# A graph layer's sorting stage: row match ahead of column match in odd steps, on TensorE and on ScalarE

## The reference

```python
h = jnp.maximum(_layernorm(x, axis=-1), 0.0)
edge_in = jnp.concatenate([h[row], h[col], dist], axis=1)   # row = src, col = dst
e = jax.nn.silu(edge_in @ eW1 + eb1)                        # 129 -> 128
e = jax.nn.silu(e @ eW2 + eb2)                              # 128 -> 128
agg = jax.ops.segment_sum(e, row, num_segments=h.shape[0])
node_in = jnp.concatenate([h, agg], axis=1)
out = jax.nn.silu(node_in @ nW1 + nb1) @ nW2 + nb2
return x + out
```

## Time and profile before

| | us |
|---|---|
| median of 3 runs | 3083.42 (3081.98 to 3084.70) |
| the profiled execution | 3085.31 |
| its span, first to last instruction | 3083.5 |
| TensorE busy (matmul) | 2661.4 (86%) |
| VectorE busy | 2136.8 (69%) |
| GpSimd busy | 2017.5 (65%) |
| ScalarE busy | 1611.0 (52%) |
| mean granted clock of TensorE | 0.984 of full speed |

### The profile page before, as it was taken

One profiled execution on the slowest core, in us unless ns is written; L12 is line 12 of the kernel. 1 busy time (PEld: TensorE's weight loads), 2 busy tenths in 40 slices (PEclk: granted clock), 3 DMA queues, 4 the chain that ended last, 5 costly groups with the idle time before them and its releaser, 6 DMA issues.

```text
span 3083.5 us, 77463 instructions
## 1 busy us (share of the span) xinstructions
PE 2661.4 (86%) x21500; PEld 2104.6 (68%) x21800; DVE 2136.8 (69%) x7363; ACT 1611.0 (52%) x3444; POOL 2017.5 (65%) x2075
## 2 busy tenths in 40 slices
PE   6899999999688888888888888888888888888898
PEld 3455555555477777777777777777777777777787
DVE  8899999898566666666666666666666666666665
ACT  3677777777344444444444444444444444444443
POOL 1244444444677777777777777777777777777772
PEclk7999999999899999999999999999999999999998
DMA  3011111111222222222222222222222222222342
GB/s 93 19 32 33 39 26 38 27 38 24 43 59 59 59 59 59 58 59 59 59 59 59 58 59 59 59 59 59 57 59 59 58 60 59 57 58 55 76 124 92
DMA packets 366119, 171.82 MB, mean 56 GB/s; under 512 B 289558, under 2 KB 330190, under 8 KB 365998
## 3 DMA queue, kind: packets, MB, share of 16 engines
q0 software_dynamic: 69600, 123.49, 15.0%
q1 hardware_dynamic: 274206, 36.33, 7.7%
q10 hardware_dynamic: 22192, 10.53, 1.2%
HBM read 139.14 MB, written 31.04 MB: 55 GB/s over the span
## 4 chain that ended last, share of the span: by engine, by line
PE 75%; issue 13%; ACT 4%; DVE 4%; POOL 3%; DMA 1%; another core or an unknown queue 0%; DVEq 0%; ACTq 0%; SPq 0%; POOLq 0%
PE bk L1216 14%; PE bk L1236 14%; PE bk L1227 13%; PE bk L1214 9%; PE bk L1204 5%; PE bk L1079 4%; POOL GA L554 3%; PE bk L1113 2%; PE bk L1145 2%; ACT BIG L1355 2%; PE bk L1067 2%; PE bk L1284 1%; PE bk L1247 1%; PE bk L1225 1%; PE bk L1068 1%
## 5 line engine op out<-in xcount | busy, mean ns | idle before, releaser
L554 POOL DMA_INDIRECT GA<-q_d,IX x1758 | 1676.5, 954 | 549.1 <-issue 532.4
L921 DVE SCALAR_TENSOR_TENSOR GA<-c_bc,EW,GA 128x128 f32<-128x128 f32 x1758 | 558.9, 348 | 437.2 <-DMA GA<-q_d,IX 433.8
L930 DVE TENSOR_TENSOR BIG<-bk,BIG 128x128 f32 x1758 | 511.6, 291 | 376.6 <-issue 156.1
L1214 PE MATMUL bk<-identf,GA 128*128 128x128 f32 x1758 | 500.9, 285 | 257.2 <-issue 240.2
L1216 PE MATMUL bk<-OHS,P 128*128 128x128 bf16 x5274 | 692.4, 225 | 0.0
L1445 ACT ACTIVATE ED<-bk,eb1c 128x512 f32<-128x512 f32 x440 | 302.2, 687 | 701.4 <-PE bk L1216 691.3
L1216 PEld LDWEIGHTS bk<-OHS,P 128*128 x5274 | 501.6, 96 | 108.0 <-issue 0.2
L519 POOL DMA_INDIRECT rec_d<-BIG,GA x208 | 245.2, 1179 | 403.3 <-issue 307.4
L1236 PE MATMUL bk<-ED 128*128 128x128 f32 x3516 | 505.7, 287 | 0.0
L1227 PEld LDWEIGHTS bk<-W,ED 128*128 128x128 f32 x3516 | 464.6, 193 | 24.4 <-issue 7.6
L1227 PE MATMUL bk<-W,ED 128*128 128x128 f32 x3516 | 465.6, 276 | 12.0 <-issue 0.7
(11 more groups left out here) (249 smaller groups left out, 2743.0 us busy)
## 6 DMA issues: line engine op xcount, KB each, us to landing
GA<-q_d,IX POOLq DMA_INDIRECT x1758, 2.5
q_d<-QS SPq DMA_DIRECT2D x14, 448.0 KB, 3.1
u_d<-QS ACTq DMA_DIRECT2D x98, 64.0 KB
OHS<-u_d SPq DMA_DIRECT2D x18, 256.0 KB, 3.0
rec_d<-ED SPq DMA_DIRECT2D x16, 220.0 KB, 9.7
RW<-rec_d SPq DMA_DIRECT2D x110, 32.0 KB
rec_d<-BIG,GA POOLq DMA_INDIRECT x208
HT<-hT_d ACTq DMA_DIRECT2D x99, 32.0 KB
```

Of the source, the lines that this page charges most:

```text
L554: e.indirect_dma_start(G[k % 4 * U + u], None, q_d, bass.IndirectOffsetOnAxis(ap=IX[g // BG % 2][:, k * U + u:k * U + u + 1], axis=0))\
L921: ins = e.scalar_tensor_tensor(out=G[k % 4 * U + u], in0=c_bc[:, :], scalar=ew[:, w:w + 1], in1=G[k % 4 * U + u], op0=ALU.mult, op1=ALU.add)
L930: e.tensor_tensor(AGG[:, ds(v, P)], banks[6 + k % 2][:, u * P:(u + 1) * P], AGG[:, ds(v, P)], ALU.add).then_inc(s["ad"], 1)
L1214: e.matmul(z, G[k * U + u], identf[:, :], is_transpose=True, start=True, stop=False)
```

## The change

In odd steps the row match is written ahead of the column match on TensorE, and the row one-hot ahead of the column one-hot on ScalarE. Even steps have no column match, and read as before. No operation, buffer or semaphore is added or removed.

```diff
                 if 0 <= v - 2 < NR:
                     place(v - 2)
+                if 0 <= v < NR:
+                    matchrow(v)
                 if v % 2 == 1 and 0 <= v + 3 < NR:
                     matchcol((v + 3) // 2)
-                if 0 <= v < NR:
-                    matchrow(v)
                 if t == NSLOT:
...
                 if 12 <= t <= 20 and t % 2 == 0 and t != 18:
                     paired({12: 0, 14: 1, 16: 2, 20: 3}[t])
+                if 0 <= v < NR:
+                    rowhot(v)
                 if v % 2 == 1 and 0 <= v + 3 < NR:
                     colhot((v + 3) // 2)
-                if 0 <= v < NR:
-                    rowhot(v)
                 for f, q, b in node.get(t, ()):
                     f(q, b)
```

## The result

The changed kernel takes 3096.75 us (median of 5 runs, 3094.28 to 3098.91), against 3082.56 us before: 1.0046 times as long, 95% interval 1.0035 to 1.0057, 14.2 us. A second set of runs gave 3098.67 against 3081.63, 1.0056 (1.0042 to 1.0069), 17.0 us.

A forecast was written before the change was run, and what follows sets the result against it. TensorE and ScalarE together were taken to bound the sorting stage. Terms -8.9 + 16.0 + 5.6 = +12.7 us on the profiled 3085.3 gave 3098.0, forecast 3096 us since that run stood 1.9 above the median; 8 in 10: 3077 to 3107.

The forecast's parts named there:

- The bound: Sorting stage: TensorE and ScalarE set the pace together, VectorE follows with some 8% of room.
- The rule by busy share: Sorting stage: the engine with highest occupancy, VectorE at 88%, sets the time, so the sum would be 0.
- The gain of even steps, 8.9 of 33.1 us: Even steps' row matches idle 33.1 us; node matmuls waiting for ScalarE's earlier pieces let only 8.9 us be kept.
- the faster rival (3073): Even steps' stalls come back whole, node matmuls not holding TensorE: -31.7 + 21.6 = -10 us, 3073 us; chance 0.15.
- The transposes, 16.0 us: Bit transposes in even steps wait 52 times for the odd step's column one-hot, now later: 16.0 us lost.
- shifted by 0.49: Column one-hot ends 0.49 us later behind the row one-hot, so bit transposes right behind it go 0.49 later.
- The three that I took off beside ScalarE's squares: Transposes in steps 48, 108, 288: squares hold the next row match anyway, so 1.5 us came off the loss.
- Odd steps, 5.6 us: Column match now stands behind the row match's wait for the even step's row one-hot: 5.6 us lost.
- It evens out: Rival: VectorE and long ScalarE pieces swallow half of the losses, +2 us, 3085 us; chance 0.20.
- the clock rival: Stalls at the squares take the granted clock down twelve more times, 12 x 1.7 = 20 us, 3116 us; chance 0.05.
- The swap was there: Answers the rival that the swap isn't there, excluded since both engines' orders show it in each of 206 steps.
- The signs named: Sorting stage 8 to 18 us longer; waits at row match more than halved, at transposes, node matmuls and VectorE's reductions longer.

The follow-up runs named there:

- node_first_elsewhere: Kernel before, row ahead of column only in odd steps not before bit transposes, ScalarE's node pieces there between the one-hots: 3066.33 against 3081.63 us, 0.9952.
- act_only: Kernel before with its TensorE order kept, row one-hot ahead of column one-hot on ScalarE alone: 3117.79 against 3081.63 us, 1.0119.
- swap_elsewhere: Kernel before, row ahead of column on both engines in odd steps except those before bit transposes: 3588.68 against 3588.65 us, 1.0001; repeated, 0.9998.
- swap_before_bits: Kernel before, row ahead of column on both engines only in odd steps whose next step has bit transposes: 3602.85 against 3588.65 us, 1.0037.
- before_again: The kernel before, unchanged, run again for a profile, on chip 12: 3081.0 us.

## Why the prediction was right, and where it was not

- **The bound.** TensorE and ScalarE together, VectorE following: right. VectorE's waits for the ladders grew by 15.2 us with the stage, and shrank by 13 when it got shorter. The rule by busy share would have had the change, node_first_elsewhere and act_only level, since none of them changes VectorE's order; they moved the time by +14 to +17, -15 and +36 us.
- **The gain of even steps, 8.9 of 33.1 us.** The mechanism is shown: the subtraction comes at the same place with and without the row match's stall, and 0.47 sooner once the pieces are moved. Its size is not confirmed by itself. What lies outside the transposes came to -6.4 and -5.1 us in the two profiles, forecast -8.9+5.6 = -3.3; in time, swap_elsewhere was level. The node pieces are indeed what the faster rival (3073) would have needed out of the way: without the transposes' loss it had -31.7+5.6, 26 us faster, and node_first_elsewhere gives 15 of them.
- **The transposes, 16.0 us.** The right place, undersized: 21.5 and 20.8 us by the trace, 14 us (9 to 18) by swap_before_bits. Why the time on chip 1 shows less than the traces of the other kind stays open. The step that failed is "shifted by 0.49". That holds where the column match could start as TensorE arrived. Where the row match is late, the old column one-hot started beside it without waiting, and the new one stands behind both:

```profile
334.18 0.39 PE L1113 MATMUL bk<-GA,ED 128*128 128x512 bf16 x1 [0.64 <-ACT BIG L1355]
334.18 0.60 ACT L1350 ACTIVATE BIG<-bk 128x512 f16<-128x512 f32 x1
...
334.93 0.27 PE L1092 MATMUL bk<-identb,ED 128*128 128x128 bf16 x2
```

```profile
339.17 0.39 PE L1113 MATMUL bk<-GA,ED 128*128 128x512 bf16 x1 [0.85 <-ACT BIG L1355]
...
340.09 0.59 ACT L1350 ACTIVATE BIG<-bk 128x512 f16<-128x512 f32 x1
...
340.82 0.27 PE L1092 MATMUL bk<-identb,ED 128*128 128x128 bf16 x2 [0.71 <-ACT BIG L1350]
```

  From row match to transposes (the timeline of before, then of after) it is 0.75 us before and 1.65 after, 0.90 lost instead of 0.49. Some five steps lose as much, of which I followed up this one. In one step, another in each profile, it is 0.6 to 0.8 higher still, and there the granted clock falls to half for 3.4 us, from 650.8 us in the first profile and from 237.5 in the second. The stretch of the first, with a granted clock of 0.66:

```profile
650.00:655.00 5.00, 4.07 (x28) 2.65 (x28) 2.87 (x6) 3.72 (x12) 1.77 (x2) 0.66 0.16 20
```

  In the first profile the 29 intervals that lose most lose 18.4 us, where the prediction had 14.2, and the other 21 lose 3.1, where it had 1.7 (3.2 less the 1.5 beside the squares). The three that I took off beside ScalarE's squares lost 0.16, 0.09 and 0.17 us: right.
- **Odd steps, 5.6 us.** No run measures this by itself; it is in the -6.4 and -5.1 above.
- **The rivals.** "It evens out" fell: VectorE swallowed nothing. The clock fell once in the stage, as before, and three times in the second profile. That is the sign that I had named for the clock rival, and the rival still fell: the two stages have the same length to 0.6 us, and the drops in steps with transposes cost 0.6 to 0.8 us, not the 1.7 that it had for each. The swap was there.
- **The signs named.** Stage 8 to 18 us longer: 15.1. L1092's wait up by 14: 14.2. L1151 and L1145 up by some 15: L1151 alone 16.2, and L1145's waits for ScalarE another 3. L1113's wait down by more than half: no, from 93 to 61 us, since the long stalls beside the squares stay.

The forecast of 3096 us for 3096.75 is thus nearer than its terms, and that is in part luck: the transposes were 5 us too low and the rest 2 to 3 us too high, which partly cancel, and the forecast was counted from 3083.4 us, where before came out at 3082.56. Against the second set's 17.0 us the 12.7 of the sum are 4 short.

## What to carry to other kernels

A stall that a swap removes is worth only the distance to the *next* thing its engine waits for. Before counting it, look up what the following instruction waits for and whether that moves too; here it hung on the same engine's queue, behind the swapped pair, and moving that brought some 10 us more on one chip and 6 on another. And an operation put second in a pair is late for all its readers: look for the reader without slack (here 52 transposes that share a bank), and swap only where there is none.

## What the runs showed of the hardware

Chip 12 and chips 1 and 15 differ by 507 to 511 us in the kernel before. A kernel of each kind of chip, compared in stretches, puts nearly all of it in the gather stage. The gathers' group on the page of before_again (chip 12) and of swap_elsewhere (chip 1), with busy time, mean ns of one, and the idle time before them with what ended most of it:

```profile
L554 POOL DMA_INDIRECT GA<-q_d,IX x1758 | 1670.9, 950 | 547.3 <-issue 533.3
```

```profile
L554 POOL DMA_INDIRECT GA<-q_d,IX x1758 | 1685.8, 959 | 1037.1 <-remote 467.3
```

and TensorE's clock and DMA from 900 to 3000 us in both:

```profile
900.00:3000.00 2100.00, 1823.79 (x15693) 1561.46 (x15693) 1333.24 (x5553) 987.82 (x1771) 1589.55 (x1674) 1.00 0.28 62
```

```profile
900.00:3000.00 2100.00, 1477.79 (x12594) 1349.43 (x12762) 1030.83 (x4509) 793.19 (x1445) 1305.46 (x1362) 0.89 0.22 48
```

A gather takes as long on the one as on the other (950 and 959 ns), but the idle time between them is nearly twice as long, 1037 us against 547, the largest part (467 us) put down to "remote", a release for which the profile has no instruction. DMA moves 48 GB/s instead of 62, and the granted clock, 1.00 in the stage on the first chip, averages 0.89. The two kernels differ in the sorting stage alone. What holds the gathers there was not tried. In the sorting stage the slower chips' profiles list 13 to 21 us of "issue" in front of the row one-hot, which chip 12's don't have. Whether that hides a gain of a few us was not shown; it is reason enough not to subtract run times of the two kinds of chip from each other.
